# A scatter loop on one core, reordered: when one-hot tiles, offset loads, weight products and clears are issued

## The reference

```
A[src, dst] += edge_weight                # 1024 x 1024, dense
deg = A.sum(axis=1); dinv = deg ** -0.5   # 0 where deg is 0
h = x
for l in range(2):                        # layer 1: two steps
    h = (dinv * A * dinv) @ h
    h = h @ W_gcn[l] + b_gcn[l]
    h = leaky_relu(h @ W_mlp[l] + b_mlp[l], 0.01)
x = layernorm(x + h)
# layer 2: two GCN convolutions with W1, W2 on the unweighted edges
# with self-loops, normalised by their counts; relu between them
x = layernorm(x + h2)
```

## Time and profile before

| | us |
|---|---|
| median of three runs (lowest to highest) | 363.85 (363.52 to 364.25) |
| the profiled execution's own time | 362.79 |
| its span | 361.0 |
| PE busy | 327.1 (91%) |
| DVE busy | 191.9 (53%) |
| ACT busy | 105.8 (29%) |
| POOL busy | 49.4 (14%) |
| mean granted TensorE clock | 0.982 |

### The profile page before, as it was taken

One profiled execution on the slowest core, in us unless ns is written; L12 is line 12 of the kernel. 1 busy time (PEld: TensorE's weight loads), 2 busy tenths in 40 slices (PEclk: granted clock), 3 DMA queues, 4 the chain that ended last, 5 costly groups with the idle time before them and its releaser, 6 DMA issues.

```text
span 361.0 us, 5012 instructions
## 1 busy us (share of the span) xinstructions
PE 327.1 (91%) x1976; PEld 266.1 (74%) x1976; DVE 191.9 (53%) x358; ACT 105.8 (29%) x183; POOL 49.4 (14%) x54
## 2 busy tenths in 40 slices
PE   2777998788949989999999999999999999999993
PEld 1555777466737878888888888888888888888882
DVE  6994676963142446103655326767690354323655
ACT  2151336242342344101344201313550355220000
POOL 2000000000010059601000001122184000000111
PEclk9998999999987999999999999999999999999998
DMA  6121003060000000000015000000700000000212
GB/s 228 27 63 58 0 7 114 3 232 4 0 3 0 0 2 0 2 0 0 2 36 196 2 0 0 3 0 2 249 17 0 0 2 0 0 4 3 87 61 87
DMA packets 8592, 13.45 MB, mean 37 GB/s; under 512 B 1906, under 2 KB 2290, under 8 KB 8564
## 3 DMA queue, kind: packets, MB, share of 16 engines
q1 hardware_dynamic: 8564, 13.05, 10.7%
HBM read 10.95 MB, written 2.10 MB: 36 GB/s over the span
## 4 chain that ended last, share of the span: by engine, by line
PE 82%; DVE 12%; issue 3%; ACT 1%; DMA 1%; DVEq 0%; POOLq 0%; POOL 0%; SPq 0%; ACTq 0%
PE psum L568 71%; PE psum L613 5%; DVE hot L912 2%; PE psum L554 2%; PE psum L601 2%; DVE wm_low L984 1%; DVE hot L909 1%; DVE wgt_low L971 1%; DVE sel L907 1%; PE psum L731 1%; DVE adj L966 1%; DMA src_i<-in_src 1%; PE psum L654 1%; PE psum L765 0%; ACT adj L403 0%
## 5 line engine op out<-in xcount | busy, mean ns | idle before, releaser
L613 PEld LDWEIGHTS psum<-hot,sel 128*128 128x128 bf16 x512 | 30.9, 103 | 17.0 <-issue 12.6
L613 PE MATMUL psum<-hot,sel 128*128 128x96 bf16 x512 | 35.6, 218 | 6.2 <-DVE hot L912 3.1
L389 POOL TENSOR_TENSOR small<-small 128x1 f32<-128x1 f32 x16 | 11.9, 742 | 162.4 <-DVE small L1135 162.4
L568 PE MATMUL psum<-at_high,x_high 128*128 128x512 f32 x64 | 26.5, 415 | 1.7 <-DVE x_low L1063 1.7
L568 PE MATMUL psum<-at_high,x_low 128*128 128x512 f32 x64 | 25.6, 401 | 0.0
L568 PE MATMUL psum<-at_low,x_high 128*128 128x512 f32 x64 | 25.6, 400 | 0.0
L971 DVE SCALAR_TENSOR_TENSOR g_low<-psum,g_high 128x512 fp32r<-128x512 f32 x16 | 10.2, 682 | 27.9 <-ACT g_high L403 27.9
L568 PE MATMUL psum<-y_high,at_high 128*128 128x512 f32 x64 | 25.0, 391 | 0.0
L568 PE MATMUL psum<-cnt,x_high 128*128 128x512 f32 x64 | 25.0, 390 | 0.0
L568 PE MATMUL psum<-y_low,at_high 128*128 128x512 f32 x64 | 24.9, 389 | 0.0
L568 PE MATMUL psum<-cnt,x_low 128*128 128x512 f32 x64 | 24.9, 389 | 0.0
(11 more groups left out here) (170 smaller groups left out, 746.6 us busy)
## 6 DMA issues: line engine op xcount, KB each, us to landing
wg_raw<-in_L_gnn_W_gcn SPq DMA_DIRECT2D x2, 1024.0 KB, 5.6
wm_raw<-in_L_gnn_W_mlp SPq DMA_DIRECT2D x2, 1024.0 KB, 6.7
x_raw<-in_x SPq DMA_DIRECT2D x1, 2048.0 KB, 9.1
xs<-in_x SPq DMA_DIRECT2D x1, 2048.0 KB, 9.1
w_raw<-in_L_gnn_W SPq DMA_DIRECT2D x2, 1024.0 KB, 6.9
out<-xs SPq DMA_DIRECT2D x8, 256.0 KB, 2.0
bias_bc<-in_L_gnn_b SPq DMA_DIRECT2D x1, 256.0 KB, 7.4
dst_i<-in_dst SPq DMA_DIRECT2D x1, 64.0 KB, 1.8
```

Source lines behind the costliest of these rows:

```text
L389: pool.tensor_tensor(r[:, 1:2], r[:, 0:1], power[:, 0:1], ALU.pow).then_inc(rstd_ready, 1)
L568: ins = pe.matmul(dest, s, m, start=first and n == 0, stop=end and n == len(pairs) - 1, skip_group_check=True)
L613: ins = pe.matmul(window(c, 1 if k == 0 else 0), stationary, moving, start=False, stop=False, skip_group_check=True)
```

## The change

- **Batches further ahead.** DVE makes batches 0, 1 and 2 before the degree operand `hw`, and a fourth one before it enters the loop. In the loop the quota is by chunk and no longer by region. The low part of a filler now stands ahead of the `make` pieces and of `add_head` of the next stop.
- **Degrees later.** The degree matmuls of chunks 0 to 15 are issued together, behind the fillers of chunk 15. They also set `batch_used` for the first three batches.
- **Fillers earlier, one at the end.** `wgt0` stands behind chunks 3, 7 and 14, the first two `wc0` tiles behind chunk 15, and so on; the last `wc1` tile stands behind chunk 127, after the loop.
- **Register loads.** Offsets are loaded into two sets of registers in turn, behind fillers, 12 times behind the first load instead of 9 times at the start of a batch.
- **Clears.** Regions 1 to 18 are cleared by two matmuls of 192 columns, which touch only the first and last 12 of each 64 columns.
- **The flag.** It is made by seven small DVE instructions instead of two, DVE loads it inside the loop, and PE no longer waits for `adj_ready` on the usual path.
- **After the loop.** `add_head` of the last region stands behind the degree sums, and the low and high parts of `x` and `at` come in the order x, at.

```diff
-        fillers = {0: [("wgt0", 0), ("wgt0", 1)], 1: [("wgt0", 2), ("wgt0", 3)], 2: [("wc0", 0)], 3: [("wc0", 1)],
...
+        fillers = {3: [("wgt0", 0), ("wgt0", 1)], 7: [("wgt0", 2)], 14: [("wgt0", 3)],
+                   15: [("wc0", 0), ("wc0", 1)], 21: [("wc0", 2)], 27: [("wc0", 3)], 34: [("bias0", 0)],
+                   40: [("biasb0", 0), ("wgt1", 0)], 47: [("wgt1", 1), ("wgt1", 2)], 53: [("wgt1", 3)],
+                   66: [("bias1", 0)], 73: [("biasb1", 0)], 79: [("wc1", 0)], 92: [("wc1", 1)],
+                   105: [("wc1", 2)], CH - 1: [("wc1", 3)]}
+        stops = sorted(set(closing) | set(fillers))
...
+                    slot = psum[:, 2 * (r % 2) + kind, :]
+                    if r in (0, NR - 1):
+                        pe.matmul(slot, none[:], zeros, start=True, stop=False, skip_group_check=True)
+                    else:
+                        ends = bass.AP(tensor=psum, offset=(2 * (r % 2) + kind) * BANK,
+                                       ap=[[8 * BANK, P], [PITCH, NB], [PITCH - WINDOW, 2], [1, WINDOW]])
+                        pe.matmul(ends, none[:], zeros[:, 0:2 * COLS].rearrange("p (h a d) -> p h a d", h=NB, a=2),
+                                  start=True, stop=False, skip_group_check=True)
...
                 if c in closing:
...
                     ins.then_inc(region_done, 1)
+                if c >= LATE_HW:
+                    ins = degree(c)
...
+                for name, i in fillers.get(c, []):
+                    filler(name, i)
+                if c + 1 in loads:
+                    load_offsets(c + 1)
...
+                if c == LATE_HW - 1:
+                    pe.wait_ge(flag_ready, 1)
                     pe.wait_ge(hw_made, 1)
-                    for k in range(first_batch):
+                    for k in range(LATE_HW):
                         ins = degree(k)
+                        if k + 1 in batch_of:
+                            ins.then_inc(batch_used, 1)
...
-            emitted = 0
-            for r in range(NR):
-                quota = min(len(later), -(-22 * r // 10) + 3)
-                while emitted < quota:
-                    make(*later[emitted])
+            for i in range(3):
+                lower_fill("wgt0", i)
+            lower_wm(0)
+            add_head(1)
+            lower_fill("wgt0", 3)
+            take_flag()
+            make_hw()
+            for k in range(5):
+                make(3, k)
+            emitted, late = 5, 5 * (NBATCH - 3)
+            for n, c in enumerate(stops):
+                if c < BATCHES[3][0]:
+                    continue
+                for name, i in fillers.get(stops[n - 1], []):
+                    if name != "wgt0":
+                        lower_fill(name, i)
+                if c == 60:
+                    lower_wm(1)
+                while emitted < min(late, 5 * (c - G) // G + 8):
+                    make(3 + emitted // 5, emitted % 5)
                     emitted += 1
...
+                if c in closing and c < CH - 1:
+                    add_head(closing.index(c))
```

More of the change, by code:

```diff
@@ L216, in gnn_resnorm @@
         ring = []
-        fillers = {0: [("wgt0", 0), ("wgt0", 1)], 1: [("wgt0", 2), ("wgt0", 3)], 2: [("wc0", 0)], 3: [("wc0", 1)],
[3 rows of a table removed]
-        filling = [t for r in range(NR) for t in fillers.get(r, [])]
-        ring += [("prep", 0, 5), ("prep", 1, 6), ("prep", 2, 7), ("prep", 3, 4), ("prep", 4, 7), ("deg", 0, 4)]
+        fillers = {3: [("wgt0", 0), ("wgt0", 1)], 7: [("wgt0", 2)], 14: [("wgt0", 3)],
[3 rows of a table added]
+                   105: [("wc1", 2)], CH - 1: [("wc1", 3)]}
+        stops = sorted(set(closing) | set(fillers))
+        filling = [t for c in sorted(fillers) for t in fillers[c]]
+        loads = [0] + [c + 1 for c in sorted(fillers) if c > closing[0] and c < CH - 1 and c != 14]
+        loads = dict(zip(loads, loads[1:] + [CH]))
+        ring += [("prep", 0, 5), ("prep", 1, 6), ("prep", 2, 7), ("prep", 3, 4), ("prep", 4, 4), ("deg", 0, 4)]
         n_fill = [0]
@@ L581, in _, with load_offsets @@
             turn(bank("prep", 3), [col_f[:]]).then_inc(prep_done, 1)
-            regs = [pe.alloc_register(f"off{j}") for j in range(G)]
+            most = max(n - c for c, n in loads.items())
+            regs = [pe.alloc_register(f"off{j}") for j in range(2 * most)]
             offsets = {}
-            def load_offsets(n):
-                b, count = BATCHES[n]
-                own = regs[:count]
-                pe.load(own, off_row[0:1, b:b + count])
+            def load_offsets(c0):
+                turns = list(loads).index(c0) % 2
+                own = regs[turns * most:turns * most + loads[c0] - c0]
+                pe.load(own, off_row[0:1, c0:loads[c0]])
                 for j, r in enumerate(own):
-                    offsets[b + j] = pe.snap(r, min_val=0, max_val=2 * BANK + REGION - 1)
+                    offsets[c0 + j] = pe.snap(r, min_val=0, max_val=2 * BANK + REGION - 1)
             def window(c, kind):
@@ L937, in take_flag @@
                 dve.wait_ge(prep_done, 5)
-                a = then(dve.tensor_reduce(max_row, bank("prep", 4)[0:1, 0:P], AX.X, ALU.max))
+                b = then(dve.tensor_copy(base_row[:], bank("prep", 4)[0:1, P:2 * P]))
+                a = then(dve.tensor_copy(step_row[:, P - 1:P], bank("prep", 4)[0:1, 0:1]))
+                after(b)
+                b = then(dve.tensor_tensor(step_row[:, 0:P - 1], base_row[:, 1:P], base_row[:, 0:P - 1], ALU.subtract))
+                after(a)
+                after(b)
+                a = then(dve.tensor_scalar(step_row[:, 0:P - 1], step_row[:, 0:P - 1], float(-WINDOW), None, ALU.add))
+                after(a)
+                a = then(dve.tensor_tensor(step_row[:], step_row[:], bank("prep", 4)[0:1, 0:P], ALU.max))
+                after(a)
+                a = then(dve.tensor_reduce(max_row, step_row[:], AX.X, ALU.max))
                 after(a)
@@ L948, in _ @@
                 make(0, k)
+            for k in range(5):
+                make(1, k)
             check_windows()
-            dve.wait_ge(spill_ready, 1)
-            make_hw()
-            for n in (1, 2):
-                for k in range(5):
-                    make(n, k)
-                if n == 1:
-                    take_flag()
-            later = [(n, k) for n in range(3, NBATCH) for k in range(5)]
+            for k in range(5):
+                make(2, k)
             def add_head(r):
```

88 lines of the change are left out of this document (34 added, 54 removed), and 3 rows, old and new, of the table fillers.

## The result

| | before | after |
|---|---|---|
| median, runs side by side (lowest to highest), us | 364.05 (363.52 to 366.24) | 369.43 (368.81 to 370.83) |
| ratio, 95% interval | 1 | 1.0156 (1.0119 to 1.0194) |
| span of the profiled execution, us | 361.0 | 367.6 |
| first `g1_a` group starts / ends, us | 108.51 / 113.24 | 116.81 / 119.79 |
| mean granted clock | 0.982 | 0.962 |

The account below looks back on a forecast made before the run. The loop was taken as a ring of PE, DVE and ACT, with PE waiting on DVE's order. New order -2.2 us, clock falls +3.8, sum +1.6 on 363.85: 365.5 us, range 360.0 to 369.5.

Parts of the forecast that it names:

- (a): Up to the first product tile: it can start at 21.9 us instead of 29.60, with PE waiting 4.9 us.
- (b): Chunks 15 to 16: batch 3 waits for degree matmuls behind two tiles, so PE waits 4.6 us at chunk 16.
- (c): Regions 2 to 7: DVE's head cycle of 4.4 to 4.9 us; waits 1.3, 0.6, 1.3, 2.0 at clears 4, 6, 8, 9.
- (d): Chunk 60: 6.9 us of DVE work between heads 7 and 8 makes PE wait 5.4 us at region 10's clear.
- (e): The wc1 tiles: low parts ahead of pieces and heads make PE wait 7.4 us at clears of regions 14, 16, 18, 19.
- the walk: Following the three engines' new lists with priced durations: loop and last tile end at 105.3 us, first g1_a group at 111.0.
- clock terms: Cost of clock falls behind long waits: 0.5 at chunk 16, 2.0 at region 10, 1.3 at three more waits; sum +3.8 us.
- each takes 1.1 us: Price of every register load on PE's sequencer; hidden behind long fillers, 2.2 us exposed in all behind short ones.
- (f): From the last tile to g1_a: it starts at 108.2 us and its first group runs 2.77 us, ending at 111.0.
- Clock cascades: Rival, chance 0.16: from chunk 60 on the clock stays low while waits of 1 to 2.7 us break work; +6, 370 us.
- The clock holds: Rival, chance 0.17: no loss of clock inside the loop, so only the walk's -2.2 us remains, 361.7 us.
- Does what its parts say: Rival, chance 0.17: DVE's order costs nothing; savings in load waits, clears and the first group's clock give -7, 357 us.

Follow-up runs that it names:

- e2: The changed kernel with the 16 late degree matmuls issued between the two wc0 tiles behind chunk 15, not behind both: 366.6 us, ratio 1.0059.
- e3: The changed kernel with 62 matmuls of 512 zero columns ahead of the long waits, to keep PE busy in them: 369.26 us, ratio 1.0121.
- e5: The changed kernel with each register load begun at the multiple of four at or below its first chunk: 368.02 us, ratio 1.0085.
- e1: The changed kernel with heads ahead of the fillers' low parts in DVE's list: 364.9 us, ratio 1.0035.
- e6: The changed kernel with heads ahead of low parts and register loads begun at multiples of four: 356.08 us, ratio 0.9737.
- e7: The changed kernel with heads ahead of low parts, loads from multiples of four, and late degree matmuls between the two wc0 tiles: 351.04 us, ratio 0.9601.
- e4: The kernel before with the small clears alone, 36 matmuls of 192 instead of 512 columns: 360.88 us, ratio 0.9895.
- e11: The kernel before with its last six register loads moved behind fillers, in two sets of 16 registers: 358.77 us, ratio 0.9852.

## Why the prediction was right in sign and wrong in size

**(a) First tile.** It started at 20.98 us (21.9 said). Right; but PE had been idle for 3.75 us ahead of it and the clock fell in the tile: two tiles took 7.30 us, not 5.7. I had let PE run at full rate. +1.6, of which the early start gave back 0.9; by chunk 16 only 0.3 was left.

**(b) Chunk 16.** Batch 3 at 28.43 (27.9 said) behind 3.32 us of idle DVE, chunk 16 at 33.40 (33.1) behind 4.71 us. Right, and e2 shows that the place of the degree matmuls is the cause of 2.8 of these 4.7 us. The clock's price behind it was 0.5 in the forecast; e3, without that low stretch, is 0.4 faster there: right.

**(c), (d) Regions 2 to 10.** The clear of region 10 came at 68.85 (67.4 said), behind 3.92 us where I had 5.4. The 5.2 us of waits at the clears of regions 4, 6, 8 and 9 were 0.44, at region 8: PE was slow behind chunk 16, and loads held it instead, 0.52, 0.64 and 2.83 us, the last at chunk 54, which I had left 0.2 to 0.6. DVE's block was on the path, so that load cost time at most through the clock. The fall came at 63.4 us, ahead of the wait of 3.92 us and not behind it as I had it; e5 with a short load fell there too and e1 with the long one did not, so its cause is open. The low clock cost 2.0 us on the path: `bias1` 3.08 us against 2.0, the clear 0.50 against 0.18 and four chunks of 0.32 to 0.38 against 0.20. I had said 2.0, and e3 won 1.8: right in size. The clock was back at 1.00 from 74 us, behind the unbroken work of chunks 63 to 66 and `bias1`.

**(e) The `wc1` tiles.** The waits of 2.41 and 2.47 us at the clears of regions 14 and 16 are those forecast (2.5 and 2.7), and e1 shows their cause. From the clear of region 10 to the last tile the walk needs 35.0 us and the forecast's clock terms 3.3; it took 42.4. Here the forecast failed. **The failed step is the clock behind these waits**: "I count half of them at 1.7 each, half of that on the path: 1.3". It fell behind both waits, each time in a tile that is on the path: 4.45 - 2.86 and 4.42 - 2.86, 3.2 us. In e1, without the waits, both tiles ran at full clock. For the second tile e3 shows what the fall cost: with the clock at 1.00, 1.3 us came back. In the third tile the fall stood over a load, and e3 got nothing back.

**The loads, the second failed term.** The forecast had "each takes 1.1 us". All loads of before start at multiples of four, so no row there could show the other price; I extended a duration to forms that it did not cover, and priced the exposed part at nothing behind product tiles. The load at 106 took 5.20 us. Under a tile at full clock 2.7 to 2.8 us of it are exposed (e3, e1), under the slow tile 1.23. From the third tile's start to chunk 106, 2.8 us are lost to the two together, and how much belongs to which is a matter of which is mended first. e6 and e7 show that these terms are no side matter: with the loads and the heads in order the same changes are worth 2.6 and 4.0%.

**What is missing, added up.** The forecast had +1.6 us and the profiles +6.6; 5.0 us are missing. Up to chunk 16 it is 0.3. In the tiles it is 3.2 - 1.3 = 1.9, and the load's 1.2 comes on top: 3.4 together. The rest is 1.6: 0.65 between chunk 16 and the clear of region 10 and 1.0 in the chunks behind it; the tail (-0.2) and the first group (+0.2) cancel.

**A reading that was wrong.** The 17.6 us of waits hold one of 2.63 us that ended at 8.40 us, ahead of the window in which the work was counted. Inside it the waits are 15.0 us, close to PE's idle time there, 15.3. So PE's work was 92.7 - 15.0 = 77.7 us and not 75.1, and 69.4 should have been 72.0. With that the sum gives 101.7 us against the walk's 96.9, and only 2.2 of the difference had a reason. The other 2.6 us are PE work that the walk does not hold, and the missing 1.6 may be part of them; no row places them.

**The sum of waits.** The walk had 27.5 us of waits, 2.2 of loads and, less the 2.2 of (a), 67.2 of work. Measured up to the last tile's end (PE alone):

```profile
8.40:114.10 105.70, 80.28 (x838) 0.87 0.14 46
```

That is 80.3 us busy and 25.4 idle. The five falls take about 11 of the busy time (my estimate: PE's busy time in each half microsecond, times the share of the clock that was missing). The work at full clock is then 69.1 us, near the 72.0 - 2.2 = 69.8 of the corrected reading. Against the forecast it is 1.9 us more, the clock 7.4 more (11.2 against 3.8) and the waits 4.3 less: 5.0. The low clock turned waits into slow work, and a sum of waits alone would have looked better than forecast.

**(f) The tail.** From the last tile to `g1_a` 5.56 us (5.8 in the walk), and the first group at full clock, 2.98 us. Right.

**Clears.** 0.17 us a pair against 0.43: 0.13 saved on each, 4.7 us, where I had taken 4.1. The rule of the Trainium skill (page "TensorE: Matmul & The Clock Gate", section "Back-to-back issue gap"), by which it was an estimated 4.8, is nearer than what I took. e4 shows 3.4 us of it on the path of before.

**The rivals.** "Clock cascades" (370 us) has the time (369.43) and half of the mechanism: low clock from 63.5 to 73.9 us and again in the second and third `wc1` tile, but it recovered each time between, and it needed the loads too. "The clock holds" (361.7 us) failed: it fell five times. "Does what its parts say" (357 us) failed for the change as made. For its parts it was modest: e4 and e11 alone gave 3.4 and 4.9 us.

## What to carry to other kernels

Price an instruction from a row only in the form in which the row shows it: where a change alters count, start or shape, keep the long end in the range and look for the place where it stands uncovered. Two losses at one place hide each other (here -0.012 and -0.007 of the ratio alone, -0.042 together), so test fixes together before dropping one. In a list written by hand put what the next engine waits for (the head) ahead of what it doesn't (low parts), and what frees a buffer ahead of long work. Here a wait of 2.5 us ahead of a product tile cost, twice, the wait and 1.6 us of low clock in the tile.

## What the runs showed of the hardware

**Register loads.** From a start at a multiple of four, four offsets cost what one costs otherwise, about 0.24 us, with some 0.1 on top: 4, 8 and 16 offsets took 0.35, 0.60 and 1.10 us before; 13 from chunk 80 took 1.13, that is three fours and one; 24 from 104 took 1.62. From other starts each costs 0.24: 13 in 3.11, 17 in 4.03, 22 in 5.20 us. (The first load of each kernel is longer: four took 0.52.) The Trainium skill, page "Runtime: NRT & Kernel Launch", section "Instruction fetch mechanics", has some 200 ns per register, and the page speaks of loads from HBM; these rows, from on-chip memory, have 237 ns at unaligned starts and 69 ns (1.10 us over 16) at aligned ones.

**The clock.** In the changed kernel it fell behind single waits of 2.41 and 2.47 us (87 and 97 us), of 2.83 (63 us) and of 3.75 (22 us), and within one of 4.71 (33 us). In e1 and e3 it also fell in stretches whose waits were 0.5 to 0.7 us, next to thin matmuls. At like waits in the changed kernel (48.9 and 53.0 us) it did not, and in e1 it stayed at 1.00 through one of 2.65 us. What tells these apart stays open. The Trainium skill's page "TensorE: Matmul & The Clock Gate", section "A second HAM failure mode: psum-queue depth-cycling", has the clock swing with short idles; the falls of e1 and e3 agree with that better than the forecast's reading, by which only the longest waits count.
